# Path attention of a two-layer model: low-rank products in four row tiles, norms by head, and another order and another engine for the short steps of the inverses

## The reference, cut to what matters

```python
w_raw = hidden @ w1.T @ w2.T              # rank 32, then 1024 columns
w_raw = silu(causal convolution over 3 tokens)
Wdir  = Ah * cos(theta) + Bh * sin(theta)
Wdir  = Wdir * rsqrt(sum(Wdir * Wdir, -1) + 1e-06)   # over the 16 channels of a head
beta  = sigmoid(hidden @ bt_w.T + bt_b) * 2.0
Mw    = strict_lower(w w^T) * beta
rhs   = strict_lower(w k^T) * beta
Bmat  = solve_triangular(Mw + I, rhs, lower=True)
logits = (q k^T - incl_lower(q w^T) @ Bmat) * SCALE
o = softmax(causal logits) @ v
```

## Time and profile before

| what | us |
|---|---|
| median of three runs | 2727.97 (2725.28 to 2741.99) |
| the profiled execution, its own time | 2729.12 |
| its span | 2727.1 |
| TensorE matmuls busy | 2386.1 (87%) |
| VectorE busy | 1476.2 (54%) |
| ScalarE busy | 940.8 (34%) |
| GpSimd busy | 589.4 (22%) |

### The profile page before, as it was taken

One profiled execution on the slowest core, in us unless ns is written; L12 is line 12 of the kernel. 1 busy time (PEld: TensorE's weight loads), 2 busy tenths in 40 slices (PEclk: granted clock), 3 DMA queues, 4 the chain that ended last, 5 costly groups with the idle time before them and its releaser, 6 DMA issues. The chain is left out here.

```text
span 2727.1 us, 66740 instructions
## 1 busy us (share of the span) xinstructions
PE 2386.1 (87%) x28984; PEld 1693.1 (62%) x28984; DVE 1476.2 (54%) x2574; ACT 940.8 (34%) x1470; POOL 589.4 (22%) x649
## 2 busy tenths in 40 slices
PE   4999999999999987999788888869769299989698
PEld 2676766766676744555455555555444188988587
DVE  5244344443434344444799999957446656666400
ACT  2233333333333321112455555532216034444211
POOL 5930000000000000000222323341030367772200
PEclk9899999999999987999899999979879589889799
DMA  2001100010000000112222232110000122221130
GB/s 73 19 21 27 32 20 20 20 38 20 20 20 20 3 24 12 30 40 76 74 74 74 80 90 88 56 53 1 0 20 18 28 46 37 45 37 48 48 147 29
DMA packets 135842, 111.17 MB, mean 41 GB/s; under 512 B 110040, under 2 KB 121197, under 8 KB 130862
## 3 DMA queue, kind: packets, MB, share of 16 engines
q1 hardware_dynamic: 135598, 107.44, 15.0%
HBM read 100.06 MB, written 7.34 MB: 39 GB/s over the span
## 5 line engine op out<-in xcount | busy, mean ns | idle before, releaser
L528 ACT ACTIVATE xa_probT<-psum,zero_column 128x1024 f32<-128x1024 f32 (+1 forms) x224 | 223.7, 1049 | 280.5 <-PE psum L376 280.5
L611 DVE COPY xa_v<-psum 128x512 f32<-128x512 f32 x96 | 66.4, 692 | 425.0 <-PE psum L353 425.0
L600 DVE TENSOR_REDUCE xa_part_max<-psum 128x2 f32<-128x802 f32 (+1 forms) x256 | 241.9, 987 | 60.4 <-PE psum L363 60.4
L353 PE MATMUL psum<-xa_wv,xa_ctxT 96*128 96x256 f32 (+1 forms) x832 | 215.8, 402 | 4.6 <-DVE xa_v L611 3.9
L374 PE MATMUL psum<-xa_qbd,xa_kT 32*128 32x128 f32 (+1 forms) x3328 | 218.6, 300 | 0.2
L345 PE MATMUL psum<-xa_ctxT,xa_wk 96*128 96x401 f32 (+1 forms) x512 | 209.1, 531 | 3.4 <-ACT xa_kT L521 1.4
L376 PE MATMUL psum<-xa_shift,xa_shift_of 32*128 32x128 f32 (+1 forms) x3328 | 208.5, 270 | 0.0
L1276 POOL TENSOR_TENSOR tk_exp_all<-tk_exp_all,tk_exp_left 128x577 f32<-128x577 f32 x64 | 120.9, 1890 | 355.1 <-ACT tk_exp_left L1397 355.1
L374 PEld LDWEIGHTS psum<-xa_qbd,xa_kT 32*128 32x128 f32 (+1 forms) x3328 | 186.6, 180 | 15.2 <-issue 5.6
L376 PEld LDWEIGHTS psum<-xa_shift,xa_shift_of 32*128 32x128 f32 (+1 forms) x3328 | 187.5, 183 | 0.0
L1444 DVE MAX8 tk_top<-tk_left 128x8 f32<-128x1601 f32 x96 | 175.1, 1824 | 4.1
(11 more groups left out here) (473 smaller groups left out, 4353.0 us busy)
## 6 DMA issues: line engine op xcount, KB each, us to landing
tk_ctx<-in_ctx SPq DMA_DIRECT2D x16, 1248.0 KB, 5.4
xa_ctxT<-in_ctxT SPq DMA_DIRECT2D x16, 1200.8 KB, 7.5
tk_ctxT<-in_ctxT SPq DMA_DIRECT2D x16, 1200.8 KB
ec_w<-in_ec_w SPq DMA_DIRECT2D x16, 1024.0 KB, 6.8
m_gate_up<-in_m_gate_up SPq DMA_DIRECT2D x17, 256.0 KB, 2.6
m_down<-in_m_down SPq DMA_DIRECT2D x17, 128.0 KB, 2.5
ff_w<-in_ff_w SPq DMA_DIRECT2D x2, 1024.0 KB
pa_m_blocks<-pa_minus_mt SPq DMA_DIRECT2D x128, 16.0 KB, 1.7
```

What stands on the lines that cost most here:

```text
L353: mm = mmul(ps[0:width(c), FILL, (c % 2) * D:(c % 2 + 1) * D], ctxT[:, h, k, c * P:c * P + width(c)], wv[:, k, :], start=(k == 0), stop=(k ...
L528: a_.activation(probT[0:w, par, u, :, 0:n], ps[0:w, at:at + 2, 0:n], ACT.Exp, bias=core.zero[0:w, :]).then_inc(e_done, 1)
L600: v.tensor_reduce(part_max[:, n, m, 2 * u:2 * u + 2], ps[:, at:at + 2, 0:z - a], AX.X, ALU.max, negate=True).then_inc(max_step, 1)
```

## The change

In the projections:

- w1 is held four times side by side, so that the factor w32 stands four times on the 128 partitions, and the four low-rank products of a group each use their own 32 rows of the array.
- raw is gone: ScalarE copies only the scaled form, and the convolution reads the plain values from PSUM. TensorE's products of the next group wait for the convolution.
- The product with the sine goes to GpSimd, the square to ScalarE.
- The norms are summed to one row a head (32 output columns, four column tiles into one bank, 256 columns each); root and reciprocal work on 256 columns, and four products spread the result over the channels of each head into banks 4 and 5, from where VectorE multiplies.
- The order of all this in the queues of TensorE, ScalarE and VectorE is written out anew.

In the batches:

- FIRST is 10 instead of 7; in odd batches, and ahead of the loop, VectorE makes the products of the steps as well as the sums. GpSimd keeps the products of steps 11 to 15 in even batches.
- VectorE takes 2 steps, maxima, shift, then masks the new matrices, 1 step, sums, adds, normalises, and the other steps.
- Three semaphores of the softmax become one.

```diff
-            w1, w2 = isb("w1", [P, KD, 32]), isb("w2", [32, 2, G, P])
-            w32 = isb("w32", [32, NT])
+            w1, w2 = isb("w1", [P, KD, P]), isb("w2", [P, G, P])
+            w32 = isb("w32", [P, NT])
...
+                for n in range(G):
+                    pool.wait_ge(s_done, n + 1)
+                    g.tensor_tensor(by(ab[:, n, 1, :]), by(ab[:, n, 1, :]),
+                                    core.filter.rotary[:, 1, :].unsqueeze(1).broadcast_to([P, B, T]), ALU.mult
+                                    ).then_inc(turned, 1)
...
+                    for c in range(4):
+                        mm = nc.tensor.matmul(ps[32 * c:32 * c + 32, 4, 0:2 * P], heads[:],
+                                              ab[:, g, 1, c * 2 * P:(c + 1) * 2 * P], start=True, stop=True)
+                    mm.then_inc(n_ps, 1)
+
+                def spread_norms(g):
+                    pe.wait_ge(n_rec, g + 1)
+                    for c in range(4):
+                        mm = nc.tensor.matmul(ps[:, 4 + c // 2, (c % 2) * 2 * P:(c % 2 + 1) * 2 * P], spread_heads[:, c, :],
+                                              norm[:, g % 2, :], start=True, stop=True)
+                    mm.then_inc(e_ps, 1)
+
+                def low_products(g):
+                    if g:
+                        pe.wait_ge(c_done, 2 * g)
+                    for q in range(4):
+                        rows = slice(32 * q, 32 * q + 32)
+                        nc.tensor.matmul(ps[:, q, :], w2[rows, g, :], w32[rows, (q % 2) * 512:(q % 2 + 1) * 512],
+                                         start=True, stop=True).then_inc(r_ps, 1)
...
+                low_products(0)
+                slabs(2)
+                low_products(1)
+                slabs(2)
+                low_products(2)
+                slabs(1)
+                norms(0)
+                slabs(1)
+                spread_norms(0)
+                low_products(3)
+                slabs(1)
+                norms(1)
+                slabs(2)
+                spread_norms(1)
                 norms(2)
+                slabs(2)
+                spread_norms(2)
+                values()
                 norms(3)
+                slabs(1)
+                spread_norms(3)
...
+                low_out(0)
+                slabs_out(2)
+                low_out(1)
+                slabs_out(2)
+                silu(0)
+                low_out(2)
+                slabs_out(1)
+                silu(1)
+                square(0)
+                roots(0)
...
+                convolve(1)
+                rotate(0)
+                convolve(2)
+                invert_norm(0)
+                rotate(1)
+                normalise(0)
...
-        FIRST = 7
+
+        FIRST = 10
...
-                for i in range(1, FIRST + 1):
-                    multiply(1, i)
                 for b in range(B):
-                    steps = steps_in(b)
+
+                    steps = [] if b % 2 else steps_in(b)
...
-                    take(3)
+                    take(1)
                     if b < B - 1:
                         level(b + 1, 4)
-                    take(3)
+                    take(2)
...
+                def step(c, i):
+                    if i <= FIRST or c == 0:
+                        multiply(c, i)
+                    add_up(c, i)
...
                     take(2)
                     if b:
                         maxima(b - 1)
-                        take(1)
                         shift(b - 1)
-                    take(2)
                     if b + AHEAD < B:
                         masked_wb(b + AHEAD, XB(b))
                     take(1)
```

## The result

The changed kernel takes 2712.68 us, the median of seven runs (2697.11 to 2721.44), beside 2727.97 us for seven of the kernel before (2725.28 to 2746.24). The ratio is 0.9918, with a 95% interval of 0.9889 to 0.9948. That is 0.8% faster, 10 us less than the predicted 2723 us and inside its range.

What follows compares the result with a forecast made beforehand. VectorE was taken to bound the projections, and in the batches even ones by VectorE's row steps, odd ones by TensorE. Projections -15 and loop +10 made -5 us, from 2728.0 to 2723 us; range 2690 to 2745, the forecast's own 2712 to 2735.

Steps and rivals of the forecast that it cites:

- Projections, -15: Projections: about 89 us from the low-rank copy on, a gain of 15 us, bounds 23 and 3.
- the layout: Projections: engine-to-engine chain in the new order, 83 us, with TensorE idle 5 us twice; lower clock adds about 6.
- PSUM charged at nothing: Projections: the convolution reading PSUM costs VectorE nothing extra; by the skill's 62 cycles, 1 us more in all.
- Start part: Between projections and loop: extra row steps fit VectorE's idle time, so it stays at 48 us, beginning about 2123 us.
- The batches without a collision: Loop: even batch 18.1 us, odd 20.1, so a pair goes from 41.0 to 38.2 us.
- The collision, 3.4 us a pair: Odd batches: VectorE's two-SBUF-input products wait 3.4 us for GpSimd's masking and spreads; the odd batch takes 23.5 us.
- The step that failed: Even batches: after TensorE idles over 4 us its clock falls, 18.1 becomes 20.5 us; pair 44.0, 3 us more.
- The rest of the loop: Loop outside the five pairs: batches 0 and 1 together +2 us, batches 12 to 14 -4.6 us.
- rival (2): Loop: collision there but the clock stays up; loop +2, projections -21, total 2709 us; chance 0.15.
- Rival (1): Loop: no collision worth the name, short products slip between; pair 38.2, loop -19, projections -18, total 2691 us; chance 0.10.
- Rival (3): Projections: narrow tiles do not overlap at 512 columns; projections only -4, total 2734 us; chance 0.05.
- Rival (4): Loop: late logits reading keeps the clock low in both batches; pair 49 us, total 2761 us; chance 0.05.

Runs made afterwards that it cites:

- wide_norms: Changed kernel with the norms as before: over all channels, root and reciprocal of 1024 columns, no spreading; 2719.08 us, ratio 0.9931.
- all_back: Changed kernel with norms, sine product and square as before, the latter two on VectorE; 2717.13 us, ratio 0.993.
- hold_pool: Changed kernel, but in odd batches GpSimd waits for VectorE's ten steps before masking the right sides; 2696.82 us, ratio 0.986.
- the run both: Changed kernel with GpSimd's wait for step 10 in odd batches and the logits read ahead of the last three steps; 2717.83 us, ratio 0.9934.

## Why the prediction was right, and where it was not

- **Projections, -15 (bounds -23 to -3).** Measured -16.0, by the predicted path. From the first low-rank product to the second block it takes 2131.9 - 2043.2 = 88.7 us, 89 forecast. Both idle times of TensorE that the layout names stand where it put them, 5.05 and 5.00 us for 5 and 5. The three runs of slabs behind idle time (6.29, 8.90 and 8.28 us where the clock's full level gives 3.70, 7.13 and 7.13) lose 5.5 us; 6 forecast. Single terms: low-rank 1.14 (1.0), reciprocal 1.75 (1.65), sine 2.63 (2.36).
- **What bounded it.** The text named VectorE's amount of work, the reciprocals above all, and let the gain follow from taking it away. On the timeline of before they do end the stage, but as the source of the gain they are small: 3 us in wide_norms, and 3 us in all_back, where all of VectorE's work is back. The size came out right because the layout in the new order was right, not because of that reason.
- **PSUM charged at nothing.** Right in the result: the 1008-column pass takes 1262 ns from PSUM and 1269 from SBUF, the product of 1024 columns that finishes w 1221 and 1224. The working was loose: it set 0.33 us from start to start beside a duration of 1.22 us, and a line of 1.04 ns a column does not pass through both with one fixed part (0.06 and 0.16 us). The 62 cycles that the Trainium skill, "VectorE: DVE Perf Modes", section on the TRN2 errata, puts on a PSUM source don't show here; the measurement decides.
- **Start part.** 48 us, measured 48.2. It begins at 2131.9 us, of which 9.8 belong to the stages ahead: 2122.1 beside the 2123 forecast.
- **The batches without a collision: 18.1 + 20.1 = 38.2 us.** hold_pool is that case: 18.6 and 19.9 on average, 38.5. (The terms that the prediction lists add up to 18.4 and 20.2, not 18.1 and 20.1; a slip of 0.4 us a pair, in which the written terms were the better ones.)
- **The collision, 3.4 us a pair.** Shown by hold_pool, and smaller: 2.6 us in the products, 2.5 in the odd batches (22.4 on average, 19.9 without). The first two steps lose time to it also (0.97 and 1.02 us for products of 2 and 8 columns), beside VectorE's idle time for the new matrices.
- **The step that failed: "its clock falls, and in the next even batch the products up to the new matrices run slower: 18.1 becomes 20.5".** The waits come, 3.4 to 4.5 us at the end of three of the pairs, but the loss behind them is smaller and not in every pair. Even batches of the five pairs take 19.0 us on average, 0.8 more than the 18.2 of the two that have no such wait in front (0.3 more than in hold_pool). The term of 2.4 us a pair was sized from the 0.58 of the earlier trace rows and charged to all pairs; measured were 0.83, 0.83 and 0.66 in three of them, and only batch 10, with 0.66 and 20.2 us, comes near the forecast's 20.5. Together with the smaller collision this makes a pair 41.3 us instead of 44.0, and the five pairs +2 us instead of +15.
- **The rest of the loop.** Batches 0 and 1 +0.3 (+2 forecast), 12 to 14 -6.6 (-4.6). Together with the pairs -4 us where +10 was forecast: the loop's change had the wrong sign.
- **The total.** -19.5 by stages. Of the cases, rival (2), the collision with the clock up, is the nearest (2709 us; loop +2, projections -21), with only 0.15. The time falls at the lower edge of the forecast's own range, 2712 to 2735, because of the loop. That it lies inside the range is in part luck: the forecast of -5 us was the sum of a projection term that held and a loop term that was 14 us off, and the range was wide enough for either sign of the loop.
- **Rival (1)**, 2691 us, has the pair that hold_pool shows, 38.2 and 38.5 us, and hold_pool's time is 2697. Its condition, short products that slip between, is false; the wait has to bring it about. **Rival (3)** is false by the 1.14 us. **Rival (4)**, slower, did not come about in the changed kernel; the run both came part of the way (42.1 us a pair, even batches 22.4), by another wait.

## What to carry to other kernels

Before a product with two SBUF inputs moves from GpSimd to VectorE, look at what GpSimd will be doing in that place: a 0.33 us product becomes 2.06 us behind a 1024-column mask, and one wait on GpSimd gives back 15 us of loop that the move had earned, a later place for three steps 11. When two repairs aim at the same delay, run them apart before together, and look at what the second now makes the first one wait for. A change of order helps only together with what makes room for it: masks three steps earlier cost 3.6 us a pair as long as eight steps stood in the even batch. An expensive instruction at the end of a stage need not be the price of the stage: with 26.2 us of reciprocals back, and norms, sine and square as they were, four fifths of the gain stayed.

## What the runs showed of the hardware

- The clock behind idle time depends on more than its length. In the kernel before it was 0.58 over 9.9 us after 2.57 us of idle time. In the changed kernel, ahead of one and the same product, it was 0.83 after 4.36 and 4.52 us, 0.66 after 3.41 and 1.00 after 2.98. In the run both, three waits of 3.14 us ahead of one product gave 0.66, 0.83 and 0.83, each over 9.9 us from the start of the wait:

```profile
2243.31:2253.21 9.90, 6.76 (x137) 6.25 (x136) 4.37 (x10) 3.23 (x10) 8.73 (x7) 0.66 0.24 24
2328.05:2337.95 9.90, 6.76 (x177) 6.49 (x176) 4.35 (x10) 3.78 (x12) 8.73 (x7) 0.83 0.27 27
2411.78:2421.68 9.90, 6.76 (x173) 6.26 (x174) 5.37 (x10) 3.77 (x12) 8.73 (x7) 0.83 0.12 14
```

  What else it depends on was not tried. A loss read at one such place is no price for all of them; it was the forecast's worst term.
- Four products with 32 rows and 512 float32 columns take 1.14 us in four row tiles, 1.99 in two and 3.87 one after the other.
- Unchanged stages differ from execution to execution: the path attention began at 2028.4 us in this profile and at 2018.6 in that of before, the mean clock over the seven runs ranged from 0.923 to 0.935, and times by 24 us. A part's gain below ten us had to be read from its own stretch.
